# Ten lookups instead of eight and Grams of two pairs at a time, in a recommendation tower on one core

## The reference

```python
e = jnp.stack([tbl_0[ids[:, 0]], ..., tbl_31[ids[:, 31]]], axis=1)    # 512 x 32 x 256, f32
dots = jnp.einsum('bnd,bmd->bnm', e, e)
z = dots[:, iu, ju]                                                    # i < j: 512 x 496
h = jnp.concatenate([z, dense_ctx], axis=1)                            # 512 x 512
h = jnp.maximum(h @ W_top1 + b_top1, 0.0)                              # W_top1: 512 x 512
h = jnp.maximum(h @ W_top2 + b_top2, 0.0)                              # W_top2: 512 x 256
y = h @ W_top3                                                         # 256 x 1
```

## Time and profile before

| | us |
|---|---|
| median of 3 runs | 164.48 |
| lowest, highest | 164.38, 165.02 |
| profiled execution, its own time | 165.76 |
| its span | 163.9 |
| PE, POOL, DVE, ACT busy | 141.8, 112.4, 91.1, 46.5 |
| mean granted clock of TensorE | 0.948 |

### The profile page before, as it was taken

One profiled execution on the slowest core, in us unless ns is written; L12 is line 12 of the kernel. 1 busy time (PEld: TensorE's weight loads), 2 busy tenths in 40 slices (PEclk: granted clock), 3 DMA queues, 4 the chain that ended last, 5 costly groups with the idle time before them and its releaser, 6 DMA issues.

```text
span 163.9 us, 7924 instructions
## 1 busy us (share of the span) xinstructions
PE 141.8 (87%) x3214; PEld 121.3 (74%) x3214; DVE 91.1 (56%) x277; ACT 46.5 (28%) x143; POOL 112.4 (69%) x124
## 2 busy tenths in 40 slices
PE   6697994999999897499999977899895699999794
PEld 6595974888878776398988865589673598898583
DVE  2191333459936568039573974367865715737642
ACT  0003010134020631205351642056460502416240
POOL 3777777777777777777777777777777777775000
PEclk9999999699999999969999999699999569999999
DMA  1699689687945843446786844433434343334000
GB/s 34 140 311 337 191 254 291 235 247 219 279 153 118 271 119 107 112 120 183 219 233 190 244 113 126 123 105 105 116 118 118 104 121 110 100 106 116 14 4 5
DMA packets 11300, 25.44 MB, mean 155 GB/s; under 512 B 2958, under 2 KB 4574, under 8 KB 11264
## 3 DMA queue, kind: packets, MB, share of 16 engines
q0 software_dynamic: 5616, 15.34, 33.0%
q10 hardware_dynamic: 4860, 9.14, 17.4%
q1 hardware_dynamic: 788, 0.46, 1.0%
HBM read 24.71 MB, written 0.00 MB: 151 GB/s over the span
## 4 chain that ended last, share of the span: by engine, by line
PE 45%; DMA 25%; POOL 13%; DVE 7%; issue 6%; ACTq 2%; ACT 1%; POOLq 0%
DMA rows<-tables,idx 24%; POOL rows L402 13%; PE xt_ps L420 12%; PE hot_ps L471 11%; PE gram_ps L435 7%; PE act_ps L501 4%; PE hot_ps L520 3%; PE dve_ps L501 3%; DVE mask L672 2%; DVE xt L337 2%; DMA ids_sb<-ids 1%; PE gram_ps L520 1%; ACTq L805 1%; DVE z L321 1%; ACTq L369 1%
## 5 line engine op out<-in xcount | busy, mean ns | idle before, releaser
L402 POOL DMA_INDIRECT rows<-tables,idx x117 | 111.6, 954 | 37.2 <-issue 26.0
L420 PE MATMUL xt_ps<-ident,rows 128*128 128x128 f32 x232 | 41.3, 292 | 12.7 <-DMA rows<-tables,idx 12.4
L420 PEld LDWEIGHTS xt_ps<-ident,rows 128*128 128x128 f32 x232 | 28.1, 148 | 18.1 <-DMA rows<-tables,idx 16.7
L471 PE MATMUL hot_ps<-mask,hot_sb 128*128 128x128 f32 x256 | 37.7, 295 | 3.3 <-ACT hot_xt L842 3.1
L337 DVE COPY xt<-xt_ps 128x512 f32<-128x512 f32 (+1 forms) x32 | 21.8, 682 | 31.0 <-PE xt_ps L420 29.1
L471 PEld LDWEIGHTS hot_ps<-mask,hot_sb 128*128 128x128 f32 x256 | 32.3, 200 | 4.6 <-issue 3.5
L435 PEld LDWEIGHTS gram_ps<-xt 128*32 128x32 f32 x1920 | 22.1, 116 | 12.8 <-issue 10.3
L435 PE MATMUL gram_ps<-xt 128*32 128x32 f32 x1920 | 29.0, 203 | 1.5 <-DVE xt L337 1.0
L348 DVE COPY last_xt<-xt_ps 128x64 f32<-128x64 f32 x28 | 7.6, 271 | 23.9 <-PE xt_ps L420 23.2
L321 ACT COPY z<-gram_ps 32x128 f32<-32x128 f32 (+1 forms) x56 | 19.4, 347 | 4.7 <-PE gram_ps L435 3.8
L321 DVE COPY z<-gram_ps 32x128 f32<-32x128 f32 (+1 forms) x56 | 19.2, 343 | 0.9
(11 more groups left out here) (70 smaller groups left out, 80.3 us busy)
## 6 DMA issues: line engine op xcount, KB each, us to landing
single_rows<-tables SPq DMA_DIRECT2D x320, 1.0 KB
hot_sb<-hot_tables ACTq DMA_DIRECT2D x8, 512.0 KB, 5.0
w_sb<-w ACTq DMA_DIRECT2D x8, 256.0 KB
rows<-tables,idx POOLq DMA_INDIRECT x117
w_packed_sb<-w_packed ACTq DMA_DIRECT2D x5, 256.0 KB
single_rows<-tables ACTq DMA_DIRECT2D x64, 1.0 KB
hot_ids_sb<-hot_ids ACTq DMA_DIRECT2D x2, 256.0 KB, 3.6
w_sb<-w ACTq DMA_DIRECT2D x1, 512.0 KB
```

Source lines behind the costliest of these rows:

```text
L402: pool.indirect_dma_start(rows[:, n % RING, :], None, tables, bass.IndirectOffsetOnAxis(idx[:, fetch:fetch + 1], 0)).then_inc(rows_landed[ ...
L420: last = nc.tensor.transpose(xt_ps[:, fetch // 2 % 2, k, fetch % 2, :], x[:, P * k:P * (k + 1)], ident[:])
L471: last = nc.tensor.matmul(hot_ps[:, k, :], hot_sb[:, l, c, P * k:P * (k + 1)], mask[:, unit % MASKS, c, :], start=(c == 0), stop=(c == HOT ...
```

## The change

- HOTS goes from (0, 4, 4, 0) to (0, 4, 6, 0): block 2 leaves out six tables. It has 26 fetches and six groups at its end (before 28 and four); there are 118 fetches, 59 pairs and 115 gathers. Ten units are looked up: four for block 1, six for block 2. Six tables are loaded, the two new ones at ACT's positions 10, 11, 13, 14, and the packed first weights move from 10 to 14 to 18 to 22.
- The first eight units take three pairs each (5, 5, 6 steps), the last two take two (8, 8); together pairs 1 to 28, as before.
- `xt` has four slots (XT_SLOTS). PE makes Grams only in even iterations, for the two pairs before; transposes wait for the copy of the pair two before. ACT's place waits for Grams four pairs back instead of two.
- Block 0's first layer goes from halves in the iterations 26 to 33 to whole parts in 29 to 32, its second layer from 35 and 36 to 34 and 35, its y from 38 to 37.

```diff
-HOTS = (0, 4, 4, 0)
+HOTS = (0, 4, 6, 0)
+XT_SLOTS = 4
...
-    for n in range(2 * N1):
-        at.setdefault(26 + n, []).append(("h1", 0, n // 2, n % 2, 2))
+    for m in range(N1):
+        at.setdefault(29 + m, []).append(("h1", 0, m, 0, 1))
...
-        for steps in (4, 4, 4, 4) if unit % 4 in (1, 2) else (5, 5, 6):
+        for steps in (5, 5, 6) if unit < 8 else (8, 8):
...
-        xt = sb("xt", [P, 2, CHUNKS, 2, QUADS, FIELDS])
+        xt = sb("xt", [P, XT_SLOTS, CHUNKS, 2, QUADS, FIELDS])
...
             for pair in range(1, PAIRS - 1):
+                if pair >= 2:
+                    pe.wait_ge(xt_ready, pair - 1)
                 for place in range(2):
                     transpose_fetch(2 * pair + place)
-                gram_pair(pair - 1)
+                if pair % 2 == 0:
+                    gram_pair(pair - 2)
+                    gram_pair(pair - 1)
                 if pair in LOOKUP_AT:
                     look_up(*LOOKUP_AT[pair])
                 mlp_at(pair)
                 set_at(pair)
-            gram_pair(PAIRS - 2)
+            for pair in range((PAIRS - 2) // 2 * 2, PAIRS - 1):
+                gram_pair(pair)
...
-                    act.wait_ge(gram_done, groups_by(pair - 2))
+                    act.wait_ge(gram_done, groups_by(pair - XT_SLOTS))
```

## The result

The changed kernel is slower, where a gain was forecast. Its median is 170.8 us (169.96 to 171.19, 6 runs), beside 165.16 us for the kernel before on the same chip: a ratio of 1.0328, 95% interval 1.0288 to 1.0367. Its profiled execution took 171.19 us, with a span of 168.7 against 163.9. The ratios in this document leave out executions more than 1.5% above the fastest of the same kernel (five of nine in e17, four of ten in e8), the medians keep them.

The account below looks back on a forecast made before the run. Gathers and closing work were taken as bounds within a microsecond or so of each other. -2.5 - 0.8 - 1.2 + 1.6 = -2.9, put at -2.5 for the rows' floor: median 164.48 to 162.0 us, 80% range 161.2 to 163.6.

Parts of the forecast that it names:

- What bounds the kernel: Gathers, one every 1.26 us, and the closing work both bound it, within a microsecond or so; PE mostly has spare time.
- Term 1: Block 2 gathers 26 times, not 28, so the last gather starts earlier: -2.5 us, if PE keeps up.
- Term 2: Pairs 1 to 28: two more units of lookups, 7.0 us of PE, are covered by its spare time: nothing.
- rival B: Around pair 29 PE is later than thought and POOL waits for its ring: up to 1.5 us more, 163.5; chance 0.1.
- term 3: From pair 48 on, four pauses ahead of Grams go: -0.8 us; over the kernel 29 pauses, 5 us.
- Term 4: Half-clock drop at 127.3 to 134.1 becomes half as long: -1.2 us (between -2.9 and +0.5), the weakest term.
- Term 5: At the end, PE's turn, second layer and last Grams wait behind ACT's dots copies: +1.6 us.
- Rival C: Waits in iterations 56 and 57 idle PE and the clock falls for the close: 166.0, by itself 165.4; chance 0.05.
- Rival D: Grams' pauses stay, belonging to waits on copies rather than the change of shape: 162.8 us; chance 0.07.

Follow-up runs that it names:

- e17: e2 with block 0's moves, weights' loads and layers of blocks 0 and 1 moved out of each other's way: 166.23 us, ratio 0.9974.
- e8: e2 with its last two units cut from 16 matmuls to 2, 56 records less (output not the reference's): 165.38 us, ratio 0.9954.
- e18: e2 with one edit, ACT's moves of block 0 two iterations later (22 to 25 instead of 20 to 23): 163.93 us, ratio 0.9949.
- e7: Kernel before plus four more matmuls in each of its eight units, 64 records in all (output not the reference's): 166.24 us, ratio 1.0057.
- e4: Changed kernel without the loads of the two added tables, lookups reading table 2's place (output not the reference's): 168.56 us, ratio 1.0244.
- e11: e2 with block 0's layers where the kernel before had them, in a session where that kernel took about 232 us: 227.48 us, ratio 0.9812.
- e16: The kernel of e11 again (e2 with block 0's layers in their old places), again in a slow session: 227.51 us, ratio 0.9821.
- e1: Kernel before with four slots of xt and two pairs' Grams together in even iterations, eight lookups kept: 166.03 us, ratio 1.0113.
- e2: Changed kernel with each pair's Grams in its own iteration again; ten lookups, 115 gathers, loads and layers as changed: 167.28 us, ratio 1.0135.
- e5: Changed kernel with one pair's Grams ahead of the even iteration's lookup and the other's behind it: 170.5 us, ratio 1.0266.
- e3: Changed kernel with ACT's packed first weights' loads at 12, 15, 18, 19, 24, last weights' one later: 168.81 us, ratio 1.0197.

## Why the prediction was wrong, step by step

**What bounds the kernel: half right.** Gathers and closing work both bounded it, and in e18 the gathers do tick at 1.26 us. What the reading missed is that PE between pairs 16 and 45 came close to being a third bound.

**Term 1 (-2.5): lost.** Two gathers went, 4.4 us of ring waits came: +1.9 at the last gather. The term said "if PE keeps up"; it didn't.

**Term 2 (0): the step that failed.** The step said that two more units are covered by PE's spare time. The amount of work was nearly so (e7). The room was wrong, in four places:
- Pair 22 to 23: "the order of those is unchanged, so that point stays". The wait did stay, but PE came to it later by up to 3.3 us, since at pair 16 PE waited twice for rows (0.98 and 0.82 us) and the clock was at half from 52.8 to 56.3 us, and ACT's copy came 3.7 us later too (70.97 against 67.23). A wait that another engine ends is no fixed point once that engine is late as well. It isn't the whole cause: in e4 pair 22 is only 0.7 us late, and pair 29 still 3.9.
- Pair 29 was taken to be 2 us late against 3.9 us of room; it was 5.0 late, and the gather at 90.43 waited 1.29. Of the 5.0, 2.2 stood at pair 24 already; the 2.8 from there on (2.8 in e4 too) are near the 2 of the sum.
- Pairs 29 to 33: block 0's first layer, moved together there, is 40 records where there were 20. By the 0.11 us of term 2 that is 2.2 us, less two pauses of 0.17; measured 1.9 (5.0 to 6.9). The sum counted this layer up to pair 29 and had no line for what moved behind it. e8 shows the same, 0.6 us late at pair 29 and 3.4 at pair 33. The layer in its old place was measured only in the sessions of 232 us (e11, e16).
- "Behind pair 33 it catches up, since it waited for rows 12.4 us in all": of the 12.4 us only 3.5 lie between pairs 33 and 44 of the kernel before, 4.7 before 28 us. A sum over the kernel was used as room at one place. PE caught up 3.2 us by pair 39, then lost 2.4 to the transfer in pair 40.

No one of these is the cause by itself. From ten lookups without shared Grams, e18 takes the wait ahead of the lookup away and the loss goes; e8 keeps that wait, takes 56 records away, and the loss goes too. Work and wait together overran the room. This is rival B's mechanism, PE late and POOL waiting, at three times its price: B allowed up to 1.5 us, and the ring took 4.4. Of these the 1.7 us at 131.41 stand behind iteration 44, and so belong to term 3, which priced long runs as short ones.

**Term 3 (-0.8; 5 us over the kernel): nothing.** The pauses went as said in e1. But a run of 64 Grams takes 0.68 to 1.5 us at full clock, not 0.70, and one of 160 takes 4.4. The sum priced 64 records from rows of 32. Over the kernel the runs grew by 6.7 us (24.6 to 31.3), more than the 5 that the pauses were to save. The Trainium skill (TensorEngine Tiling (Array Packing), Key Properties) says that a change of tiling mode drains TensorE; the runs agree that a pause of 0.17 us stands ahead of a run of Grams, and show that fewer of them were worth nothing here.

**Term 4 (-1.2): the length right, the price not shown.** The drop at 127.3 to 134.1 became one of 3.4 us, as taken. Elsewhere the kernel before has drops of 3.4 us at 28.3, 69.2 and 103.4, and the kernel after one of 3.4 at 52.8 and one from 110.9 to 117.7: the same 10.2 us, at other places. A drop of 3.4 us in a span of 163 lowers the mean clock by 0.01. In e8, where PE is late, the ten executions lie nearly in order of this mean, from 163.4 us at 0.979 over 165.5 at 0.958 to 168.4 at 0.939, some 1 us for each 0.01. The executions of the kernel before range from 164.7 us on average at 0.979 to 165.5 at 0.948, only 0.3 us for each.

**Term 5 (+1.6): right.** 15.57 - 13.8 = 1.8 us, through the very wait named. e2 without the shared Grams has 13.8, and e1 with them, at 60 pairs, 13.8 as well.

**Rival C** did not happen: the clock stayed at full through the close. **Rival D** was refuted by e1.

**What stays open.** Between the spans of e2 and the kernel after lie 3.2 us, of which the end is 1.8. The other 1.4 are what e5, without the long run, is earlier at pair 56; but e5 differs from the kernel after at pair 23 and in the close too, so it doesn't isolate them. The edit of e18 was tried neither on the kernel with the Grams together nor on the kernel before.

What stops the loads isn't settled either. The Trainium skill (TensorE: Matmul & The Clock Gate, the section on the array of 16 times 32x32) gives TensorE a queue of 64 instructions, as many as the loads and matmuls of 32 records. But runs of 32 stood still in the same place too, 0.51 us in e2 and 0.71 in e18, so that number by itself doesn't draw the line. The trace holds another trail: its DMA records show transfers of 16 KB of instructions (queue q8 of the page, 25 in the kernel after). In the traces of the 165-us sessions the loads of Grams pause seven times for 0.5 us or more, and each of these pauses ends 2.3 to 2.7 us after such a transfer starts: in the kernel after it starts at 124.77 and the pause ends at 127.21, in e2 at 120.10 and 122.58, in e18 at 118.34 and 120.97. That would fit loads that wait for their own instructions. No run tests it.

## What to carry to other kernels

Room is local: before work is called covered, add up the waits between the place where it is added and the first place where lateness costs something, not over the whole kernel. When PE is to carry more, look first at its longest wait for another engine and at what stands in that engine's queue ahead of the awaited instruction; here DMA issues two iterations later gave back 3 us to ten lookups, more than they had lost. Try such an edit on the kernel before as well, or its gain is put down to the change. A saving on an engine that follows another is only worth what it does at the places where that engine is late.

## What was unexpected of the hardware

- 32-column weight loads go at 11 ns each at first, 32 in 0.35 us, and in longer runs they falter, mostly from the 42nd record on: 64 take 0.68 to 1.5 us, 160 in a row 4.4.
- PE waits 2.5 to 3.8 us for ACT's copy in ten of the traces of the 165-us sessions, and in eight of them a fall to 1.2 GHz starts within or behind this wait (3.4 us in e2, a mean clock of 0.66 over 5.0 us). The kernel after and e3 have the wait without the fall; e17 and e18 have neither.
- The same kernel before takes 165 us in most sessions and 232 in two. In the latter the traces of its variations show PE's loads held back inside runs of 32 (0.63 us of 1.44), and ten lookups win 2 to 3%, while e2 loses 1.35% in the others.
